# The last text layer's gain moved ahead of the row scale on GpSimd, and a layer's weight splits done a step earlier

## The reference, cut to what matters

```python
def _layer(x, W_in_l, cw, cb, WB, WC, Dv, Wo, g, b):
    x_in, x_gate = split(x @ W_in_l.T)            # 256 -> 2 x 512
    u = silu(depthwise_conv4(x_in) + cb)
    Bu = u @ WB.T                                 # 512 -> 64
    hs = scan(h = 0.95 * h + 0.05 * bu)           # along the 77 tokens
    y = (hs @ WC.T + Dv * u) * silu(x_gate)
    z = y @ Wo.T + x
    return (z - mean(z)) * rsqrt(var(z) + 1e-05) * g + b
```

## Time and profile before

| | |
|---|---|
| time, median of 3 runs | 1261.61 us (1259.63 to 1265.9) |
| the profiled execution's own time | 1266.81 us |
| its span, first to last instruction | 1264.6 us |
| TensorE busy | 1072.6 us, 85% |
| VectorE busy | 744.1 us, 59% |
| GpSimd busy | 614.6 us, 49% |
| ScalarE busy | 546.1 us, 43% |
| TensorE's mean granted clock | 0.911 of full speed |

### The profile page before, as it was taken

The page is one execution under the profiler, slowest core; times in us unless marked ns, Lnnn a source line. Parts: engine busy times, 40 slices in busy tenths (PEclk is TensorE's granted clock), DMA queues, the critical chain, the costliest instruction groups (busy, mean ns, idle before and its releaser), DMA issues.

```text
span 1264.6 us, 21028 instructions
## 1 busy us (share of the span) xinstructions
PE 1072.6 (85%) x5958; PEld 862.6 (68%) x5959; DVE 744.1 (59%) x1918; ACT 546.1 (43%) x1202; POOL 614.6 (49%) x662
## 2 busy tenths in 40 slices
PE   5569999999999999786589698369999999999930
PEld 3459999999999999786456466336666666666620
DVE  2587888888888887665478598612222222222238
ACT  1337776777677776343045254012222222222224
POOL 5515666666666666445533366723333332332336
PEclk8888999999999999888788698579999999999975
DMA  9320001000100000111059412322222222222254
GB/s 245 114 88 1 2 1 60 1 2 2 59 2 2 1 2 1 37 40 36 15 194 376 119 42 57 89 53 46 42 46 46 42 46 45 46 45 43 46 127 126
DMA packets 54289, 75.36 MB, mean 60 GB/s; under 512 B 10081, under 2 KB 47711, under 8 KB 53321
## 3 DMA queue, kind: packets, MB, share of 16 engines
q1 hardware_dynamic: 31712, 48.92, 12.4%
q0 software_dynamic: 16640, 18.50, 9.0%
q10 hardware_dynamic: 5865, 7.05, 2.1%
HBM read 45.30 MB, written 29.11 MB: 59 GB/s over the span
## 4 chain that ended last, share of the span: by engine, by line
PE 75%; DVE 7%; issue 6%; POOL 4%; DMA 4%; ACT 3%; DVEq 0%; SPq 0%; another core or an unknown queue 0%; POOLq 0%; ACTq 0%
PE bank L1326 18%; PE bank L1076 16%; PE bank L1140 11%; PE bank L1342 9%; PE bank L1135 4%; PE bank L1334 2%; PE bank L1225 2%; DMA xrows<-arena_b,slot_i 1%; DMA arena_b<-in_patches 1%; PE bank L1104 1%; PE bank L1124 1%; PE bank L1125 1%; PE bank L1112 1%; POOL xrows L986 1%; PE bank L1228 1%
## 5 line engine op out<-in xcount | busy, mean ns | idle before, releaser
L1326 PE MATMUL bank<-arena_a,arena_b 128*128 x512 | 234.7, 601 | 0.8 <-ACT arena_b L819 0.6
L997 POOL DMA_INDIRECT yrows<-arena_b,dest_i x64 | 99.7, 1558 | 269.0 <-ACT arena_b L831 261.3
L1463 DVE SCALAR_TENSOR_TENSOR arena_b<-bank,sml,arena_b 128x304 f32<-128x304 f32 (+2 forms) x384 | 195.9, 523 | 25.4 <-ACT arena_b L671 22.9
L1076 PE MATMUL bank<-xt_hi,w_hi 128*128 128x308 f32 x512 | 161.7, 316 | 10.3 <-DVE arena_b L1463 5.3
L1780 DVE TENSOR_TENSOR arena_b<-bank,arena_b 128x512 f32<-128x512 f32 x64 | 44.3, 692 | 200.0 <-PE bank L1326 200.0
L1326 PEld LDWEIGHTS bank<-arena_a,arena_b 128*128 128x128 f32 x512 | 92.8, 191 | 97.7 <-issue 94.2
L1076 PE MATMUL bank<-xt_hi,w_lo 128*128 128x308 f32 x512 | 158.5, 310 | 0.0
L1076 PE MATMUL bank<-xt_lo,w_hi 128*128 128x308 f32 x512 | 158.1, 309 | 0.0
L912 POOL TENSOR_TENSOR u_halves<-arena_b,u_halves 128x308 fp32r<-128x308 f32 x128 | 109.1, 863 | 95.4 <-ACT arena_b L683 95.4
L906 POOL TENSOR_TENSOR y_lo<-arena_b,y_hi 128x308 fp32r<-128x308 f32 x128 | 107.6, 853 | 37.6 <-ACT y_hi L695 37.4
L1342 PE MATMUL bank<-arena_a,arena_b 128*128 x512 | 121.3, 380 | 1.2 <-DVE arena_b L1792 0.9
(11 more groups left out here) (173 smaller groups left out, 2280.9 us busy)
## 6 DMA issues: line engine op xcount, KB each, us to landing
arena_b<-xrows SPq DMA_DIRECT2D x64, 129.0 KB
arena_a<-in_w_gate SPq DMA_DIRECT2D x1, 4096.0 KB
arena_a<-in_w_up SPq DMA_DIRECT2D x1, 4096.0 KB
arena_a<-in_w_down SPq DMA_DIRECT2D x1, 4096.0 KB
h_all<-seq SPq DMA_DIRECT2D x8, 448.0 KB
arena_b<-in_patches SPq DMA_DIRECT2D x10, 324.0 KB
w_raw<-in_w_in SPq DMA_DIRECT2D x3, 1024.0 KB
yrows<-padbuf SPq DMA_DIRECT2D x2, 1440.0 KB
```

Of the source, the lines that this page charges most:

```text
L997: pool.indirect_dma_start(yrows, bass.IndirectOffsetOnAxis(ap=dest_i[:, k:k + 1], axis=0), f_y[k], None, compute_op=ALU.add).then_inc(y_se ...
L1076: mm = pe.matmul(out_, in_half(w, layer, d, slice(c * P, (c + 1) * P)), x[:, d, cols], start=(k == 0), stop=(k == len(pairs) - 1))
L1326: mm = pe.matmul(bank[q][:, :], x_gt[k][:, d, :], w[:, d, bass.ds(e * FFN, FFN)], start=(d == 0), stop=(d == DC - 1))
L1463: dve.scalar_tensor_tensor(acc[:, :, back_:TXT], x[:, :, 0:TXT - back_], conv_w(s // GROUPS, c, tap), acc[:, :, back_:TXT], ALU.mult, ALU. ...
```

## The change

Two edits. In the last text layer the product with the norm's gain becomes a call of its own, `keep_gain(t)`, and stands ahead of `row_scale(o)` in GpSimd's iteration; the sum with the bias stays where both stood. It keeps its waits: for the normed rows, and for the stores that read the same buffer two steps before. The weights' parts are no longer spread one to a step over steps 2 to 7 of a layer: steps 2 to 5 have one, step 6 has two, and step 7 none. ScalarE and GpSimd take them in the same places within a step as before.

```diff
-        def split_part(g):
-            return bass.ds(g * SPLIT_COLS - 2 * SPLIT_COLS, SPLIT_COLS)
+        def split_part(k):
+            return slice(k * SPLIT_COLS, (k + 1) * SPLIT_COLS)
+
+        SPLITS_AT = {2: (0,), 3: (1,), 4: (2,), 5: (3,), 6: (4, 5)}
+        def next_splits(a):
+            return SPLITS_AT.get(a % GROUPS, ()) if turns(a) else ()
...
-                if live(a) and a < KEEP and a % GROUPS >= 2:
-                    split_weights(a // GROUPS + 1, split_part(a % GROUPS))
+                for k in next_splits(a):
+                    split_weights(a // GROUPS + 1, split_part(k))
...
-            def keep_rows(t):
+            def keep_gain(t):
                 g = t - KEEP
-                rows = kept[g % 2]
                 pool.wait_ge(rows_n, t + 1)
                 wait(pool, seq_stored[2 + g % 2], 16 * PIECES * (g // 2))
-                pool.tensor_tensor(rows, n, gb_s[:, 0:1, :].broadcast_to([TR, NT, D]), ALU.mult).then_inc(pool_ng, 1)
+                pool.tensor_tensor(kept[g % 2], n, gb_s[:, 0:1, :].broadcast_to([TR, NT, D]), ALU.mult).then_inc(pool_ng, 1)
+
+            def keep_rows(t):
+                g = t - KEEP
                 pool.wait_ge(pool_ng, g + 1)
-                pool.tensor_tensor(rows, rows, gb_s[:, 1:2, :].broadcast_to([TR, NT, D]), ALU.add).then_inc(rows_kept, 1)
+                pool.tensor_tensor(kept[g % 2], kept[g % 2], gb_s[:, 1:2, :].broadcast_to([TR, NT, D]), ALU.add)\
+                    .then_inc(rows_kept, 1)
 
             def text_step(i, a, b, o, t):
                 if live(o):
                     lower_half(o, 1)
                     lower_half(o, 2)
                     lower_half(o, 3)
+                if live(t) and not turns(t):
+                    keep_gain(t)
+                if live(o):
                     row_scale(o)
                 if i == STEPS + 1:
                     norm_ahead(0)
-                if live(a) and a < KEEP and a % GROUPS >= 2:
+                for k in next_splits(a):
                     layer = a // GROUPS + 1
-                    split_weights(layer, split_part(a % GROUPS), layer * SPLITS + a % GROUPS - 1)
+                    split_weights(layer, split_part(k), layer * SPLITS + k + 1)
```

More of the change, by code:

```diff
@@ L437, in build @@
         assert SPLIT_COLS * SPLITS == W_COLS
-        def split_part(g):
-            return bass.ds(g * SPLIT_COLS - 2 * SPLIT_COLS, SPLIT_COLS)
+        def split_part(k):
+            return slice(k * SPLIT_COLS, (k + 1) * SPLIT_COLS)
+        SPLITS_AT = {2: (0,), 3: (1,), 4: (2,), 5: (3,), 6: (4, 5)}
+        assert sorted(k for at_ in SPLITS_AT.values() for k in at_) == list(range(SPLITS))
+        def next_splits(a):
+            return SPLITS_AT.get(a % GROUPS, ()) if turns(a) else ()
         def in_half(half, layer, d, cut):
@@ L920, in lower_turned @@
                     .then_inc(xt_split, 1)
+            def keep_gain(t):
+                g = t - KEEP
+                pool.wait_ge(rows_n, t + 1)
+                wait(pool, seq_stored[2 + g % 2], 16 * PIECES * (g // 2))
+                pool.tensor_tensor(kept[g % 2], n, gb_s[:, 0:1, :].broadcast_to([TR, NT, D]), ALU.mult).then_inc(pool_ng, 1)
             def keep_rows(t):
                 g = t - KEEP
-                rows = kept[g % 2]
-                pool.wait_ge(rows_n, t + 1)
-                wait(pool, seq_stored[2 + g % 2], 16 * PIECES * (g // 2))
-                pool.tensor_tensor(rows, n, gb_s[:, 0:1, :].broadcast_to([TR, NT, D]), ALU.mult).then_inc(pool_ng, 1)
                 pool.wait_ge(pool_ng, g + 1)
-                pool.tensor_tensor(rows, rows, gb_s[:, 1:2, :].broadcast_to([TR, NT, D]), ALU.add).then_inc(rows_kept, 1)
+                pool.tensor_tensor(kept[g % 2], kept[g % 2], gb_s[:, 1:2, :].broadcast_to([TR, NT, D]), ALU.add)\
+                    .then_inc(rows_kept, 1)
             def text_step(i, a, b, o, t):
```

## The result

The changed kernel takes 1223.26 us (median of 4 runs, 1213.7 to 1226.05) against 1263.76 of the kernel before (4 runs, 1259.63 to 1272.75). The forecast was 1217 against 1261.61, a ratio of 0.9646, in a range of 1209 to 1229.

The account below looks back on a forecast made before the run. The last text layer's steps were taken to be bound by the wait for GpSimd's product alone. Savings of 29.4 + 7.35 + 3.0 + 2.0 + 2.9 = 44.65 us against the median 1261.61 gave 1217 us, range 1209 to 1229.

Parts of the forecast that it names:

- The wait passed along: Last text layer: VectorE's row norm waits 35.7 us for GpSimd's product, TensorE 30.2 us for that norm; one wait.
- The four full steps: Last text layer: four steps of 22.05 us each become 14.70, saving 29.4 us; bounds 21 and 29.4.
- a sign of being wrong: Among the signs against the prediction: a TensorE wait at L1135, for the row norm, of over 0.5 us.
- The product free in the gap: GpSimd, last layer: the product, some 1.82 us, fits the idle 3.96 us before VectorE's moments and costs the row scale nothing.
- rival A: Last layer: a small wait stays, as with a product slowed beside busy VectorE; 1.5 us in six steps, 1226 us; chance 0.16.
- The sum and the stores: GpSimd's sum stays last and costs nothing; stores need 4.2 us, and the product reusing their buffer comes 18.4 us later.
- The clock: Last layer: loss of 7.35 us a step exceeds the 5.26 wait; granted clock is 0.50 over 2.89 us behind it.
- Rival B: Last layer: waits go but the clock stays low, or another wait long enough to lose it stays; 1228 us; chance 0.08.
- The end of the text part: Last step to the attention: last sum about 2 us earlier, attention norm beside three GpSimd operations; 2.0 us, bounds 0 and 4.5.
- The splits: Layer starts: TensorE's waits for the weights' low halves go, 2.9 us; doubled part costs 0, bounds 0 and 0.2 a layer.
- idle times like the 0.76: Step with two parts: GpSimd's extra 1.27 us goes into idle times like 0.76 us and the next steps' 3.96.
- What was let pass: Attention and experts behind the text part read the same data in the same order, so they shift whole, unchanged.

Follow-up runs that it names:

- gain_x2: The changed kernel with the product made twice into the same place, one after the other; 1222.68 us, ratio 0.9679 to the kernel before.
- gain_x3: The changed kernel with the product made three times into the same place; 1232.12 us, ratio 0.9747 to the kernel before.
- one_kept: The changed kernel with one buffer, not two, for the last layer's rows, so each product waits for the stores of the step just before; 1220.33 us, one run.
- gain_behind_scale: The changed kernel with the product directly behind the row scale, not ahead of it; 1230.24 us, ratio 0.9738 to the kernel before.
- gain_behind_u: The changed kernel with the product behind the low half of u (chunk 0); 1244.26 us, one run.
- gain_behind_y: The changed kernel with the product behind the low half of y (chunk 0); 1244.46 us, ratio 0.9848 to the kernel before.

## Why the prediction was right, point by point

**The wait passed along.** Right, and shown from both sides: with the product early VectorE no longer waits for it (35.7 us before), TensorE's 30.2 us are down to one wait of 1.2, and each place further back brings back a wait on TensorE (1.0, 1.8, 3.25, 5.27 us). The four full steps, 29.4 us, and the fifth, 7.35, came to 29.38 and 7.31. The four could be sized that well because the trace of before held one step of the same instructions without the wait. That the fifth came so near is partly luck: it has fewer products, and was given the mean of the four. The one wait left, 1.21 us in the sixth step, is over the 0.5 us that the prediction names as a sign of being wrong; but its own sum leaves 4.07 less 3.0, about 1.1 us, there.

**The product free in the gap.** Right: 1.85 us, 2.21 us left. gain_x2 and gain_x3 show the gap's size, about 4 us plus some 0.6 of slack behind it. Its time beside a busy VectorE, 1.85 us, is nearly that beside a waiting one, 1.80, so the contention in rival A did not come.

**The sum and the stores.** Right; the landing is not one number: read in the same way from SP's queue it takes 4.2, 4.5 and 4.1 us in three steps of the kernel before and 5.1 and 4.5 in two of the changed one, 5.1 in the step of one_kept above. All are covered.

**The clock.** Right in size for the kernel before and after. Rival B put the loss at waits of some 5 us; the runs show it from 1.8 us on in the full steps. In the sixth step, which has two waits close together (1.88 and 1.21 us), it is lost in the changed kernel too.

**The end of the text part.** Its mechanism was right and its size low: 3.2 us against 2.0. The last two row norms are 11.88 us apart and were 16.29, 4.4 us more. Of this 3.2 us are the last one's wait, 1.32 us for the row scale where it was 4.54 for the product. With the attention norm 1.2 us slower, as reckoned, that makes the 2.0. The other 1.2 us were not in the sum for this stretch: from the residual's start to the statistics TensorE takes 7.75 us (575.01 to 582.76) and took 8.94 (614.29 to 623.23), with the same instructions at a higher mean clock, 0.79 against 0.67.

**The splits.** The start of a layer gives 1.25 us, where I took the 0.97 of the wait alone: the 0.3 us that a wait costs beyond its idle time count here too. The doubled part costs 0.33, where I took 0 with a bound of 0.2. The step of the argument that failed is the one that sent GpSimd's extra 1.27 us into "idle times like the 0.76": the first such idle time stands behind the `lower_turned` that ScalarE waits for. Three times 1.25 less 0.33 is 2.8, so two errors of opposite sign gave the forecast's 2.9, which is luck.

**What was let pass.** That attention and experts shift whole is true on the whole, but between the two profiles of the changed kernel the attention differs by 5 us, the experts by 1 and the start of the text part by 2.6, and the start differs by up to 10 us between chips. The text part came out 0.9 us better than forecast. So the difference between 1217 and 1223.26 lies outside it: 2 us are the kernel before's own median (1261.61 in the first three runs, 1263.76 in four, 1263.57 to 1267.61 in the later sets), and the other 4 are within that scatter, though no run shows them one by one.

## What to carry to other kernels

Where an engine waits at the same point of each step, that gap is a place for work whose inputs are old and whose result is wanted early. Size the gap from the trace, and put the work ahead of the wait, not behind it: the same split cost 1.25 us at a layer's start, 0.33 doubled a step earlier, and nothing in the gap. When a wait is passed along from engine to engine, look for a step of the same work without it; its length prices the removal, clock included, better than the sum of the waits does.

## What the runs showed of the hardware

TensorE's clock fell behind a wait far shorter than the 5.3 us of the kernel before, and not each time. With idle times of 1.8 us, once a step and otherwise full, the granted clock over the 3 us behind was 0.66 in one step and 1.00 in the next, at a cost of 1.5 us or none; with 3.25 us it was 0.57, 0.70 and 1.00 in the first three steps; with 1.0 us it was always 1.00. Over the four full steps and the fifth of each profile the clock was lost behind none of ten waits of 0.7 to 1.3 us (gain_x3, gain_behind_scale), two of five of 1.8 to 2.1 (gain_behind_u), four of five of 3.2 to 3.5 (gain_behind_y) and all five of 5.1 to 5.3 (the kernel before). The sixth step stands apart: there two waits close together, 1.88 and 1.21 us in the changed kernel, were enough. The Trainium skill (TensorE: Matmul & The Clock Gate, What's actually happening) says that the window over which TensorE's activity is judged runs free of the kernel, which would let equal waits end differently; the runs agree in that, and do not show the window itself.

VectorE's norm over SBUF data (four instructions) took 1.37 us alone and 5.36 us beside three elementwise operations of GpSimd, while the row norm, which reads PSUM, took its 1.45 us beside GpSimd's sum too. One by one the four took 1.60, 1.90, 1.70 and 0.40 us: three of them about as long as the GpSimd operations beside them (1.56, 1.87 and 1.54 us), which kept their usual times. In one_kept, where GpSimd's second operation comes later, only the first is slow (1.60 us) and the norm takes 2.57. Here it was VectorE that paid.
